# Product-key experts: the residual is added by TensorE and copied out by ScalarE instead of being added by VectorE

## The reference

```python
xn = rmsnorm(x); q = (xn @ w_q.T).reshape(b, t, H, 2, DK)      # H = 8 heads
sim1, sim2 = q . keys                                          # 32 scores each, per head
s1, s2 = top_k(sim1, 8), top_k(sim2, 8)
fs, pk = top_k(s1 + s2 for all 64 pairs, 8)                    # 8 of 1024 experts per head
hidden = gelu(xn . expert_down[fi]) * relu(fs)
out = sum over heads and chosen experts of hidden * expert_up[fi]
x = x + out
```

## Time and profile before

| | |
|---|---|
| median of 3 runs | 2717.45 us |
| profiled execution | 2717.39 us, span in the trace 2715.5 us |
| first product-key layer (names k5a) | about 1639 to 2114 us of the span |
| second product-key layer (k7a) | about 2229 to 2705 us |
| whole span: VectorE, TensorE, ScalarE, GpSimd busy | 83%, 78%, 68%, 61% |

### The profile page before, as it was taken

The page is one execution under the profiler, slowest core; times in us unless marked ns, Lnnn a source line. Parts: engine busy times, 40 slices in busy tenths (PEclk is TensorE's granted clock), DMA queues, the critical chain, the costliest instruction groups (busy, mean ns, idle before and its releaser), DMA issues. The chain is left out here.

```text
span 2715.5 us, 59525 instructions
## 1 busy us (share of the span) xinstructions
PE 2108.9 (78%) x17482; PEld 1769.0 (65%) x17483; DVE 2266.1 (83%) x5568; ACT 1859.9 (68%) x4284; POOL 1647.9 (61%) x1502
## 2 busy tenths in 40 slices
PE   5648888869599999694588877888888348888887
PEld 2236666768488888683466656777777227777776
DVE  6589999865488888656888857999999779999997
ACT  3579999736555555363255548899898339999996
POOL 0069999627400000375556648999999219999996
PEclk9869999969799999697699988999999669999999
DMA  2023333141200000111100000000000000000001
GB/s 59 3 53 97 97 97 97 60 141 52 64 1 0 0 0 1 45 51 43 40 3 0 0 1 1 0 0 0 0 0 0 0 0 1 0 0 0 0 0 31
DMA packets 67735, 70.66 MB, mean 26 GB/s; under 512 B 10264, under 2 KB 46320, under 8 KB 67504
## 3 DMA queue, kind: packets, MB, share of 16 engines
q1 hardware_dynamic: 61488, 57.56, 7.4%
q0 software_dynamic: 4992, 10.23, 1.4%
q10 hardware_dynamic: 1120, 1.22, 0.2%
HBM read 57.32 MB, written 11.67 MB: 25 GB/s over the span
## 5 line engine op out<-in xcount | busy, mean ns | idle before, releaser
L1893 POOL TENSOR_TENSOR k7a_psums<-k7a_sims 128x1024 f32<-128x1024 f32 x224 | 421.4, 1914 | 18.3 <-DVE k7a_w L2101 14.1
L1893 POOL TENSOR_TENSOR k5a_psums<-k5a_sims 128x1024 f32<-128x1024 f32 x224 | 421.4, 1913 | 18.3 <-DVE k5a_w L2101 14.1
L980 POOL TENSOR_TENSOR mc_hc<-mc_h,mc_cs 128x512 f32<-128x512 f32 x256 | 327.5, 1296 | 34.0 <-DVE mc_h L947 17.3
L1958 PE MATMUL k7a_pw<-g_ident,k7a_w 128*128 128x128 f32 x2048 | 265.5, 277 | 72.6 <-DVE k7a_hid L2110 48.2
L1958 PE MATMUL k5a_pw<-g_ident,k5a_w 128*128 128x128 f32 x2048 | 265.5, 277 | 72.2 <-DVE k5a_hid L2110 47.9
L1958 PEld LDWEIGHTS k7a_pw<-g_ident,k7a_w 128*128 128x128 f32 x2048 | 226.8, 141 | 115.9 <-DVE k7a_w L2101 52.6
L1958 PEld LDWEIGHTS k5a_pw<-g_ident,k5a_w 128*128 128x128 f32 x2048 | 226.8, 141 | 115.4 <-DVE k5a_w L2101 52.5
L947 DVE TENSOR_TENSOR_SCAN mc_h<-mc_dA,mc_inj 128x512 f32<-128x512 f32 x256 | 298.5, 1200 | 2.2 <-PE mc_inj L836 1.8
L2101 DVE SCALAR_TENSOR_TENSOR k7a_w<-k7a_psums,k7a_best,k7a_lift 128x1024 f32<-128x1024 f32 x224 | 279.2, 1271 | 0.5 <-ACT k7a_lift L2029 0.3
L2101 DVE SCALAR_TENSOR_TENSOR k5a_w<-k5a_psums,k5a_best,k5a_lift 128x1024 f32<-128x1024 f32 x224 | 279.2, 1271 | 0.5 <-ACT k5a_lift L2029 0.3
L2029 ACT ACTIVATE k7a_lift<-k7a_psums 128x1024 f32<-128x1024 f32 x224 | 228.4, 1020 | 35.3 <-DVE k7a_w L2101 31.1
(11 more groups left out here) (525 smaller groups left out, 5958.5 us busy)
## 6 DMA issues: line engine op xcount, KB each, us to landing
mc_cs<-c_rows SPq DMA_DIRECT2D x128, 256.0 KB, 3.1
e_w<-in_L_ffn_W_dram SPq DMA_DIRECT2D x16, 256.0 KB, 5.8
token_rows<-e_zn SPq DMA_DIRECT2D x16, 256.0 KB, 3.4
e_zn<-token_out SPq DMA_DIRECT2D x16, 256.0 KB, 5.2
g_X<-in_L_attn_a_x_dram SPq DMA_DIRECT2D x8, 256.0 KB, 5.7
out_dram<-g_X SPq DMA_DIRECT2D x1, 2048.0 KB, 8.7
e_zs<-token_rows,e_token POOLq DMA_INDIRECT x78, 2.6
token_out<-e_ys,e_token POOLq DMA_INDIRECT x78, 2.3
```

Source lines behind the costliest of these rows:

```text
L980: nc.gpsimd.tensor_tensor(hc[:, q % RH, :], h_[:, q % RB, :], cs[:, S % RC, :], ALU.mult).then_inc(outs, 1)
L1893: nc.gpsimd.tensor_tensor(psums[:, h - 1, :, :], rows_of(p, h), s2, ALU.add).then_inc(pooled, 1)
L1958: ins = nc.tensor.matmul(pw[:, j, :], w[:, h % WR, j * P:(j + 1) * P], env.ident[:, :], start=(h == 0 and j % 4 == 0), stop=(h == HD - 1 a ...
```

## The change: what it does

The sum `x + out` is made in PSUM. `out` begins with one more matmul, the identity against the old tile of `X`, which starts the accumulation; the eight matmuls on `hid` add to it. ScalarE, no longer VectorE, moves the result: a copy from `pmix` to `X`, placed after `gate(t+1, 0)` and ahead of `raise_(t, 5)`. VectorE keeps `statistics`, one weighing later, after `weigh(t, 6)`. The semaphore `added`, which `statistics`, `sim` and `out` wait for, is now raised by ScalarE.

```diff
                     need(pe, added, t)
+                    nc.tensor.matmul(pmix[:, 0:P], env.ident[:, :], env.X[:, t, :], start=True, stop=False)
                     for j in range(J):
-                        ins = nc.tensor.matmul(pmix[:, 0:P], hid[:, j, :], up[:, j, :], start=(j == 0), stop=(j == J - 1))
+                        ins = nc.tensor.matmul(pmix[:, 0:P], hid[:, j, :], up[:, j, :], start=False, stop=(j == J - 1))
                     ins.then_inc(made, 1)
...
+                def residual(t):
+
+                    hold(act, made, t + 1)
+                    nc.scalar.copy(env.X[:, t, :], pmix[:, 0:P]).then_inc(added, 1)
...
                         if not final:
                             gate(t + 1, 1 - p, 0)
+                        if not begun:
+                            residual(t - 1)
                         raise_(t, 5)
...
                 rounds(act, NT // 2, body)
+                residual(NT - 1)
...
-                def residual(t):
-
-                    need(dve, made, t + 1)
-                    nc.vector.tensor_tensor(env.X[:, t, :], env.X[:, t, :], pmix[:, 0:P], ALU.add).then_inc(added, 1)
...
                         weigh(t, p, 5)
+                        weigh(t, p, 6)
                         if not begun:
-                            residual(t - 1)
                             statistics(t - 1)
-                        weigh(t, p, 6)
                         weigh(t, p, 7)
 
                 rounds(dve, NT // 2, body)
                 finish(NT - 1, 1)
-                residual(NT - 1)
                 statistics(NT - 1)
```

More of the change, by code:

```diff
@@ L2033, in body @@
                         t = it * 2 + p
-                        final = last and p == 1
+                        begun, final = first and p == 0, last and p == 1
                         raise_(t, 0)
```

## The result

| | before | changed |
|---|---|---|
| median | 2718.3 us (4 runs) | 2804.63 us (4 runs, 2802.04 to 2806.57) |
| ratio, 95% interval | 1 | 1.0312 [1.0299, 1.0325] |
| span of the profiled execution | 2715.5 us | 2803.6 us |
| VectorE busy, 1650 to 2050 us | 391.41 of 400 us | 353.85 of 400 us |

The account below looks back on a forecast made before the run. Two loops of nearly one length, one on VectorE, one over VectorE and TensorE, were taken to bound the kernel at 14.46 us a tile. 2717.4 + 80.4 = 2797.8, forecast 2797 us, range 2787 to 2822, widened downward to 2768.

Parts of the forecast that it names:

- The wait on ScalarE: ScalarE's copy, ahead of the relu of head 5, waits 1.6 us for `out`, making each tile 1.28 us longer.
- T: End of VectorE's weighing of head 2 in a tile; the prediction's times are measured from it.
- The two times that no row of before showed: End of `out` to start of ScalarE's copy, taken as 0.15 us; start of copy to start of relu, 0.25 us.
- The sum: Both product-key layers: 62 tiles x 1.28 = 79.4 us, with about 1 us more for the layers' last tiles.
- The clock: Rival, 5%: TensorE's clock also falls to its lower level in a tenth of the tiles, 50 us more, 2847 us.
- TensorE's passes: The identity matmul's two passes at the start of `out`: 0.22 us a tile, on the chain with nothing beside them.
- the rival that counts them alone: Rival, 8%: ScalarE's stand is absorbed, only TensorE's two passes stay on the chain: 14 us, 2731 us.
- The rival in which VectorE sets the pace: Rival, 4%: the chain through TensorE is misread and each tile is 0.49 us shorter: 30 us, 2687 us, faster.
- the second loop: Loop over VectorE and TensorE, from the weighing of head 2 through `finish` and top-8 back, read as 14.46 us.

Follow-up runs that it names:

- e1: Changed kernel with ScalarE's copy moved behind the relu of head 7: 2727.58 us, ratio 1.0022 to the kernel before.
- e4: Kernel before without VectorE's addition, leaving out the residual of both product-key layers: 2711.69 us, ratio 0.9961.
- e3: Kernel before with the identity matmul added and VectorE copying where it added: 2728.58 us, ratio 1.0028.
- e2: Changed kernel without the identity matmul, leaving the old rows of X out of the sum: 2785.78 us, ratio 1.0238 to the kernel before.
- f4: Kernel before with the top-8 moved behind the weighing of head 2 and VectorE's addition left out: 2690.78 us, ratio 0.9890.
- f2: Kernel before with only VectorE's top-8 moved behind the weighing of head 2, GpSimd's candidates moving too: 2722.68 us, ratio 1.0010.
- g1: Changed kernel with four more matmuls, result unused, on TensorE ahead of the transposes of head 0: 2795.34 us, ratio 1.0285 to the kernel before.

## Why the prediction was right

**The wait on ScalarE.** Right in place and size. The steps, predicted and measured, from T: end of `out` 3.15 and 3.16; copy 3.30 and 3.35; relu of head 5 3.55 and 3.52; relu of head 6 5.56 and 5.53; weighing of head 6 6.63 and 6.57; `finish` 10.58 and 10.52. A tile 15.74 and 15.67 us. The two times that no row of before showed came out at 0.19 us (end of `out` to the copy, taken as 0.15) and 0.17 us (copy to the relu, taken as 0.25). e1 shows that this wait, with the relus queued behind it, is the cause: 77 of 86 us go with it (6 of them are the tiles at the lower clock).

**The sum.** 62 tiles x 1.28 us = 79 us were predicted; the tiles gave 1.21 us, 75 us. The two layers, first to last `finish`, grew by 40.7 and 42.2 us, 82.9 us in all. The difference is the twelve tiles at the lower clock, 12 x 0.5 = 6 us, and some 2 us at the ends. The rest of the 88.1 us by which the spans differ lies ahead of the first product-key layer, in code that is the same: its input rows were made at 1629.3 us in this execution and at 1624.5 in the one of before. Between the experiments' executions, all with the same code there, this point lay anywhere from 1625.7 to 1629.9, so it is no effect of the change.

That 2797 came within 8 us of 2804.63 is in part luck. The tiles were 4 us shorter than predicted, the clock added 6 us that the sum left out, the ends 1 us, and 5 us came from ahead of the layer.

**The clock.** The rival had a chance of 5% and a price of 50 us. Its mechanism came true together with the forecast's, not in its place, at an eighth of the price. The step that was mis-sized is the cost of a tile at the lower level: I took all 74 passes at that level, 8 us; only sixteen transposes and a few more passes were, and most of that stood beside VectorE's top-8, 0.5 us. How often it happened was too low instead: a tenth of the tiles was assumed, and it was a fifth.

**TensorE's passes.** "They stand on the chain with nothing beside them" was wrong as a reading of the kernel before. e4 gives that loop as 14.34 us, 0.12 less than VectorE's own, so the first 0.12 us were free: the rival that counts them alone would have cost 62 x 0.11 = 7 us, as e3 shows (0.28%), and not 14. In the changed kernel the error had no effect, for with ScalarE in the loop all of the 0.22 counts (e2).

**The faster side.** The rival in which VectorE sets the pace was right about the kernel before and wrong about the worth of it: 0.49 us less on VectorE brings 0.12 (e4), since the second loop is right behind. Only with the top-8 moved does the whole come through (f4: 14.46 - 13.99 = 0.47).

## What to carry to other kernels

Before work is given to an engine with time to spare, see that its input is ready when its turn comes. Here ScalarE kept its order and turned one early wait into a delay for everything queued behind it; here the place of a 0.27 us copy decided between 1.0312 and 1.0022. So for a moved instruction write down when its input is ready and what is queued behind it, before asking how busy the engine is.

When two loops through the engines are of nearly one length, relieving either alone shows little or nothing and looks like a failed idea. Measure each loop's length by taking work out of the other, and change them together: f2 gave 1.0010, e4 0.9961, both together 0.9890.

## What the runs showed that I had not expected

A piece that the chain of waits shows as one can hide a wait: sixteen transposes of 1.87 us on the chain were 1.76 us of work and 0.11 us of waiting, and those 0.11 us told which loop was the longer.

A kernel can win by giving TensorE work to throw away: with eight more passes a tile (g1) the two layers of the changed kernel took 6.5 us less, since the twelve tiles at the lower clock level were gone.
